# The routing blocks of a fused attention and mixture-of-experts kernel moved behind the row maximum in their VectorE slots

## What is computed

```
xn = layernorm(x)
q = rope(xn @ wq);  c_kv = xn @ w_down;  k, v = split(c_kv @ w_up);  k = rope(k)
attn = softmax(causal(q k^T / sqrt(128))) @ v @ wo
scores = sigmoid(xn @ gate_w.T);  top_scores, top_idx = top_k(scores, 2)
combine = one_hot(top_idx) * 2.5 * top_scores / sum(top_scores)
y[e] = (silu(xn @ w1[e]) * (xn @ w3[e])) @ w2[e];  routed = sum_e y[e] * combine[e]
shared = (silu(xn @ sw1) * (xn @ sw3)) @ sw2
out = x + attn + routed + shared
```

## Time and profile before

| | |
|---|---|
| Median of 3 runs | 722.88 us (722.71 to 723.11) |
| The profiled execution | 723.37 us |
| Its span, first to last instruction | 721.3 us |
| TensorE busy / VectorE busy / ScalarE busy / GpSimd busy | 694.9 / 631.5 / 603.6 / 546.0 us |
| Slots 0 to 4, from the block of slot 0 to behind that of slot 4 | about 60.9 to 112 us of the span |

### The profile page before, as it was taken

One profiled execution on the slowest core, in us unless ns is written; L12 is line 12 of the kernel. 1 busy time (PEld: TensorE's weight loads), 2 busy tenths in 40 slices (PEclk: granted clock), 3 DMA queues, 4 the chain that ended last, 5 costly groups with the idle time before them and its releaser, 6 DMA issues.

```text
span 721.3 us, 15694 instructions
## 1 busy us (share of the span) xinstructions
PE 694.9 (96%) x4536; PEld 625.5 (87%) x4536; DVE 631.5 (88%) x1765; ACT 603.6 (84%) x1513; POOL 546.0 (76%) x498
## 2 busy tenths in 40 slices
PE   5798989999999999999999999999999999999997
PEld 4686878888898999999999999999999999998886
DVE  6868989999998889889888988988888898889996
ACT  4577777887887899899989889888998989889984
POOL 3455576778875778888888788888788878988881
PEclk9799999999999999999999999999999999999999
DMA  9553423444335455656457555655656655522103
GB/s 296 183 178 111 159 84 118 155 132 131 105 125 165 129 158 128 199 140 165 118 141 211 130 152 140 177 154 136 168 125 179 163 140 143 132 45 65 61 1 117
DMA packets 65571, 100.28 MB, mean 139 GB/s; under 512 B 9712, under 2 KB 38992, under 8 KB 65488
## 3 DMA queue, kind: packets, MB, share of 16 engines
q1 hardware_dynamic: 58048, 89.70, 40.3%
q0 software_dynamic: 7152, 9.34, 7.7%
q10 hardware_dynamic: 288, 0.26, 0.1%
HBM read 70.50 MB, written 28.78 MB: 138 GB/s over the span
## 4 chain that ended last, share of the span: by engine, by line
PE 77%; DVE 11%; ACT 5%; issue 3%; POOL 3%; DMA 1%; DVEq 0%; ACTq 0%; POOLq 0%
PE qk_proj L490 15%; PE scores L490 14%; PE u_acc L490 14%; PE out_acc L490 11%; PE ffn L490 9%; PE probs_t L596 8%; ACT swapped L857 2%; DVE rot L1350 2%; PE ffn L682 2%; PE ffn L656 1%; DVE acc L1406 1%; DVE rot L1357 1%; ACT split L849 1%; DVE scores L1366 1%; POOL swapped L1041 1%
## 5 line engine op out<-in xcount | busy, mean ns | idle before, releaser
L1041 POOL TENSOR_TENSOR swapped<-swapped,sin_t 128x512 f32<-128x512 f32 x128 | 167.5, 1309 | 117.4 <-DVE rot L1357 86.4
L1056 POOL TENSOR_TENSOR qk_lo<-rot,qk_hi 128x512 fp32r<-128x512 f32 x128 | 164.8, 1297 | 10.8 <-ACT qk_hi L866 7.6
L1381 DVE TENSOR_TENSOR pt_lo<-probs_t,pt_hi 128x512 fp32r<-128x512 f32 x238 | 117.5, 494 | 47.9 <-ACT pt_hi L888 47.4
L857 ACT ACTIVATE swapped<-qk_proj 64x512 f32<-64x512 f32 x256 | 151.7, 593 | 7.9 <-PE qk_proj L490 3.3
L877 ACT ACTIVATE probs<-scores,nbias 128x512 f32<-128x512 f32 (+3 forms) x256 | 134.7, 527 | 23.1 <-DVE nbias L1366 21.5
L888 ACT ACTIVATE pt_hi<-probs_t 128x512 fp32r<-128x512 f32 x238 | 104.8, 440 | 30.8 <-PE probs_t L596 19.4
L1366 DVE CUSTOM_DVE_ANT_0 scores<-scores,mask 128x512 f32<-128x512 f32 (+3 forms) x256 | 125.3, 489 | 4.5 <-PE scores L490 2.2
L1406 DVE SCALAR_TENSOR_TENSOR acc<-out_acc,rsum,acc 128x256 f32<-128x256 f32 x256 | 111.1, 476 | 6.0 <-PE out_acc L490 3.6
L596 PE MATMUL probs_t<-ident,probs 128*128 128x128 f32 x604 | 105.5, 273 | 3.2 <-DVE pt_lo L1381 2.9
L1350 DVE TENSOR_TENSOR rot<-qk_proj,cos_t 128x512 f32<-128x512 f32 x128 | 87.4, 683 | 10.2 <-ACT swapped L857 9.3
L490 PE MATMUL scores<-qk_hi 128*128 128x512 f32 (+3 forms) x256 | 93.4, 365 | 1.4 <-ACT probs L877 1.1
(11 more groups left out here) (195 smaller groups left out, 1927.8 us busy)
## 6 DMA issues: line engine op xcount, KB each, us to landing
wt<-expert_parts SPq DMA_DIRECT2D x39, 704.0 KB, 4.5
wt<-expert_parts SPq DMA_DIRECT2D x39, 512.0 KB
raw_a<-in_attn SPq DMA_DIRECT2D x8, 768.0 KB, 5.0
xs_sorted<-u_lo SPq DMA_DIRECT2D x3, 1677.0 KB, 8.0
xs<-xs_sorted SPq DMA_DIRECT2D x39, 129.0 KB, 2.5
expert_parts<-split SPq DMA_DIRECT2D x8, 352.0 KB, 2.3
expert_parts<-raw_f SPq DMA_DIRECT2D x8, 352.0 KB, 2.4
ys_tokens<-mask SPq DMA_DIRECT2D x1, 2176.0 KB, 8.3
```

Of the source, the lines that this page charges most:

```text
L857: last = ac.activation(swapped[64 * half:64 * half + 64, which, :], qk_bank[64 - 64 * half:128 - 64 * half, :], ACT.Copy)
L1041: pool.tensor_tensor(swapped[:, which, :], swapped[:, which, :], sin_t[:, :], ALU.mult).then_inc(sinm_ok[which], 1)
L1056: pool.tensor_tensor(qk_lo[:, m % 2, which, :], rot[:, which, :], f32(qk_hi[:, m % 2, which, :]), ALU.subtract).then_inc(rlo_ok[which], 1)
L1381: ve.tensor_tensor(pt_lo[:, c], turn_bank(m, j)[:, 0:n], f32(pt_hi[:, c]), ALU.subtract).then_inc(ptlo_ok, 1)
```

## The change

In the VectorE program, `pt_parts(s, 3)` and `row_max(s + 2, 3)` are issued ahead of the routing blocks in place of behind them. In instructions these are three: the subtraction, the maximum and the read of its accumulator. Nothing else is moved, and in slots without a block the order is what it was.

```diff
                     expert_parts(n)
                 sorted_parts(f)
+                pt_parts(s, 3)
+                row_max(s + 2, 3)
                 if s == PICK_AT:
                     route_scores()
                     route_best(0)
...
                     place_rows()
                 if s == PLACE_AT + 2:
                     place_owners()
-                pt_parts(s, 3)
-                row_max(s + 2, 3)
                 rotate(s + 3, 0)
                 cos_product(s + 3, 1)
                 gate_h(f)
```

## The result

The changed kernel takes 722.16 us (median of 22 runs) against 723.13 us for the kernel before in 22 runs beside it: a ratio of 0.9987, interval 0.9981 to 0.9992, so 0.94 us faster (0.6 to 1.4). That is less than the 0.2% that I had called distinguishable, and only the many runs make it certain. The profiled execution took 722.15 us, its span 720.0.

A forecast was written before the change was run, and what follows sets the result against it. Bound by TensorE and what makes it pause, with routing blocks on the path in slots 0, 2 and 3. Slot 2 (-0.49 + 0.13 = -0.36) and slot 3 (-0.36) make 722.88 - 0.72 = 722.16, rounded 722.2 us; range 721.2 to 723.3.

The forecast's parts named there:

- The order costs nothing by itself: Slots 0 to 4, VectorE: block and pair take the same sum in either order; the earlier maximum gains 0 us.
- Two held operations: L1314 in slot 2 and the first L1320 in slot 3, held by GpSimd, are freed: 0.49 and 0.36 us less.
- The new waits: The moved pair waits for its scores in slot 2: +0.13 us in sum, bounds 0 and +0.5 over five slots.
- Nothing absorbs it: Slots 2 and 3 gain 0.36 us each, kept to the end unless GpSimd's pause at 90.04 takes slot 2's.
- The sum: Slot 2 -0.36 us, slot 3 -0.36, slots 0, 1 and 4 nothing: -0.72 us, from 722.88 to 722.16.
- The bound on the good side: ScalarE's earlier start may save 0.3 us in each of slots 1 and 4, making -1.3 us in all.
- The slower rival: The pair waits for late scores, with block, rotate and g queued behind: 725 us and more; chance 0.10.

The follow-up runs named there:

- slots 0, 1, 4 only: Against the kernel before, the pair goes ahead of the block in slots 0, 1 and 4 only: 722.62 us, ratio 0.9996.
- the added products: The changed kernel with three GpSimd products added behind wa_lo in slot 1, 1024 columns in all: 723.17 us, ratio 1.0003 to the kernel before.

## Why the prediction was right

- **The order costs nothing by itself.** Right. The pair took 60.84 to 61.64, 0.80 us as estimated, and slots 0, 1 and 4 kept their lengths within 0.02 us. TensorE's and ScalarE's gains ahead of `g` went into a longer wait for `g`. What I missed: ScalarE's head start in slot 1 reaches GpSimd, and would have freed most of L1314 on its own (slots 0, 1, 4 only).
- **Two held operations.** Right in place, cause and size: 0.49 and 0.36 us, shown by three kernels that change only GpSimd: in the old order both operations are free once its subtractions are short, and in the new order L1314 is held again once it has reads to do there. What the prediction's rows didn't show is that `tensor_scalar` is held with one SBUF operand; there is none in the moved pair.
- **The new waits.** Right: 0.13 us in slot 2, none in the others.
- **Nothing absorbs it.** Right: the pause of GpSimd at 90.04 moved along, and the shift of 0.76 us stayed to the end, where the 0.32 us near 220 us came on top.
- **The sum.** 0.72 us forecast; the trace has 0.76 from the named cause and 0.32 from a pause of VectorE that I hadn't looked at, together 1.08, and the runs 0.94 (0.6 to 1.4). That the median of 722.16 fell on the forecast is in part chance: the kernel before came out at 723.13 in the longer series, and not at the 722.88 from which I had subtracted. And 0.32 us of the gain come from something that the prediction didn't have.
- **The bound on the good side** (0.3 us each in slots 1 and 4 from ScalarE) had no basis: those slots gave nothing. The additional gain came from elsewhere.
- **The slower rival** was weighed rightly, and its price looks better than it is. Made real with scores 0.52 us late, it should by the prediction's rule cost 5 x 0.52 - 0.72 = 1.9 us, and the ratio of 1.0026 is 1.9 us. That is luck. VectorE waited in four slots, not five, for 1.63 us in all, half of the runs lost only 0.8 us, and the profiled one of the other half lost 1.5 us in one slot to TensorE's clock, which the prediction didn't count.

## What to carry to other kernels

Before moving an operation of VectorE, look at what GpSimd does at the old and at the new place. An operation whose duration is well above that of its own shape elsewhere, beside a GpSimd operation that reads SBUF, is held. Here these were operations with two SBUF operands and `tensor_scalar` with one. An operation that reads PSUM and at most one SBUF operand can stand there in its place. Then check whether the one put ahead has its inputs in time. And measure the shift of each slot between fixed points of two traces: it told 0.3 us apart where medians scatter by more than one.

## What the runs showed of the hardware

**When the hold ends.** In six cases (L1314, L1320, L1415 before; L1314 with slots 0, 1, 4 changed, 84.63 + 0.39 - 0.29 = 84.73 against 84.86; L1314 and L1296 beside the added products) VectorE was released 0.13 to 0.15 us before the end of the GpSimd record. L1260 in slot -1 has 0.16 (57.98 + 0.79 - 0.24 = 58.53 against 58.68). Where several GpSimd operations followed each other, beside the added products, it was held by the one in flight alone.

**Where the scatter of the runs comes from.** The 22 runs of the changed kernel reach from 720.6 to 723.2 us. They fall into groups by the mean granted clock: five runs at 0.998 average 721.0 us, thirteen at 0.992 or 0.993 average 722.5. The windows of its two profiles, in the start phase, show where (first 720.0 us span, then 719.1):

```profile
24.00:30.00 6.00, 2.90 (x6) 1.83 (x6) 5.73 (x17) 2.47 (x8) 2.50 (x2) 0.61 0.93 293
30.00:36.00 6.00, 5.23 (x17) 4.29 (x18) 4.63 (x11) 4.21 (x7) 3.45 (x4) 0.54 0.34 116
```

```profile
24.00:30.00 6.00, 2.81 (x6) 1.74 (x6) 5.69 (x18) 2.31 (x7) 2.32 (x2) 0.76 0.91 282
30.00:36.00 6.00, 4.19 (x22) 3.54 (x23) 4.67 (x12) 4.26 (x8) 3.63 (x4) 0.95 0.39 127
```

TensorE is idle for half of the window from 24 us, its clock goes to the lower level, and in one execution it stays there to 36 us and in the other it is back soon after 30. The same program, 1.1 us apart by 57 us of the span. A change of less than 0.2% has to be read with that in mind. The kernel before has both ends too: of its 94 runs beside the experiments five have 0.998 and average 721.8 us, 47 have 0.993 and average 723.4. At equal clock the changed kernel is thus 0.8 to 0.9 us faster. It reached 0.998 more often, in 5 of 22 runs, which helps its median, and no run shows whether that is chance.
